# A second attention in fixed slots: one PSUM bank for inputs, one for results, later evictions, and one layer norm in place of two

## The chip, the core and the metric

The kernel runs on one core of a Trainium2 chip (trn2). The metric is device time in microseconds of one execution, the median of the runs shown. Engines are named as the profile names them: PE is TensorE (PEld its weight loads), DVE is VectorE, ACT is ScalarE, POOL is GpSimd, SP is SyncE, which issues most of the DMAs.

## The reference, cut to what matters

Four blocks in a row on x of shape (16, 256, 256): an attention with shared keys (L0), a mixture of 8 experts with the two best taken (L0), a second attention (L1), and a permuted set of small experts (L1). The change touches the third block, and the end of the second, which the kernel has merged into it. The outer layer norm and the one inside the attention follow on each other, with nothing between them:

```python
x = x + _L0_ffn_ref(_layernorm(x), ...)          # y rows of two experts, weighted, added to x
x = x + _L1_xattn_ref(_layernorm(x), ctx_1024, ...)

def _L1_xattn_ref(x, context, ln_gamma, ln_beta, w_q, w_kv, w_out, b_out, gate):
    xn = _layernorm(x, ln_gamma, ln_beta)         # eps 1e-5, as the outer one
    q = (xn @ w_q)                                # 16 heads of 64
    k, v = split(context @ w_kv)
    attn = softmax(q * 64**-0.5 @ k^T)            # per head 256 x 256
    out = (attn @ v) @ w_out + b_out
    return out * tanh(gate[0])
```

## The kernel before, in words

The work is cut into phases with a meeting of all engines between them (`phase_end`, L189). The phase concerned is the second attention: `pe_l1` (L1125), `dve_l1` (L1185), `act_l1` (L1268), `pool_l1` (L1292), `sp_l1` (L1325). Keys and values of all 16 batch entries were projected earlier and lie in DRAM. X (4096 x 256, fp32) stays in SBUF. A batch entry ("a batch" below) has 256 rows, that is two tiles of 128, and 16 heads, taken as 8 pairs. There are U = 128 pairs in all, and the loop runs over pairs; one turn of it is a slot.

For a pair u the steps are, in order: `s`, the scores (PE, 12 matmuls into two of three banks, L1139); the row maxima out of those banks (DVE, two instructions, L214); `e`, the exponentials with row sums (ACT, four instructions, L225); `g`, the reciprocals (DVE, L232) and the division by the sums (POOL, one instruction of 128 x 1024, L238); `t`, the transposes (PE, 8, L248) and their eviction (ACT, two, L255); `pv`, the product with the values (PE, 8 records, L1153) into bank 5, which DVE empties in two instructions, a rounded high part (L1225) and the rest (L1227). Matmuls whose operands are split into a high and a low part run as three products.

Once per batch there is other work. The expert rows are gathered by POOL (4 indirect DMAs, L1296) and added to X by DVE (`ca`, 4 instructions, L1192). Row statistics follow (`stats_dve`, L150: two of L153, two of L157, three small ones) and a reciprocal square root by three Newton steps on POOL (`newton_pool`, L167, 12 small instructions). Step `cm` normalizes into XN1 and takes statistics of the normalized rows, with a second `newton_pool`; step `p1` normalizes again, twice per tile (four instructions of L184). Then `p1b` transposes XN1 (PE, 4, L1161), scales it out of PSUM (DVE, L1244), rounds it (L1249), and POOL makes the low part (L1318). The query projections `q` come in 4 groups of 12 matmuls (L1171); ACT evicts the high part (L1286), DVE the low part (L1253). The keys `kk` are split by ACT (L1290) and POOL (L1323) in 4 parts. The results `o` of a batch are two groups of 24 matmuls (L1181), one per tile; DVE adds the bias (L1260), then gate and residual (L1263), and the statistics for the next phase.

`schedule` (L57) writes one list of steps, `seq1` (L1109), and every engine walks it in this order. The per-batch steps wait in a list `pend` and are dealt out in thirds over the places in a slot; a batch's two `o` steps go to the front of that list once its last `pv` is in. In a slot the order is `s`, `g` of the pair before, pieces, `e`, `t` of three pairs before, pieces, `pv` of four pairs before, pieces. So DVE empties a pair's values in the slot in which PE makes them, and the next row maxima stand behind that. Banks 7 and 6 serve the per-batch steps in turn (`mbank`, L144; `m1`, L1118).

Of the kernel before, what the change touches and what calls it, by code (L numbers as in the profile page):

```python
# [14 lines left out]
U = 128  # L15
EPS = 1e-5
# [40 lines left out]
def schedule(ins, outs, late):  # L57

    seq = [s for _, s in ins(0)]
    pend = deque()  # L60

    def pieces(n, at):
        while n > 0 and pend and at >= pend[0][0]:
            seq.append(pend.popleft()[1])
            n -= 1

    for i in range(U + 4):
        if i < U:
            if i % 8 == 0:
                pieces(len(pend), i)  # L70
                if i // 8 + 1 < 16:
                    pend.extend(ins(i // 8 + 1))
            seq.append(("s", i))
        if 1 <= i <= U:
            seq.append(("g", i - 1))
        n = -(-len(pend) // (8 - i % 8))
        pieces(n // 3 + (n % 3 > 0), i)
        if i < U:
            seq.append(("e", i))
        if 3 <= i <= U + 2:  # L80
            seq.append(("t", i - 3))
        pieces(n // 3 + (n % 3 > 1), i)
        if i >= 4:
            seq.append(("pv", i - 4))
            if (i - 4) % 8 == 7:
                for s in reversed(outs((i - 4) // 8)):
                    pend.insert(min(len(pend), late), (0, s))
        pieces(n // 3, i)
    pieces(len(pend), i)
    return seq  # L90


def build(nc, A, OUT):
# [33 lines left out]
    MV2 = keep("MV2", [128, 32, 2], fp32)  # L127
    RSTD = keep("RSTD", [128, 32], fp32)
    RSTD2 = keep("RSTD2", [128, 32], fp32)
# [17 lines left out]

    s_st, s_nw = sem("ln_guess"), sem("ln_newton")

    def stats_dve(e, w, k, t0, n, mv, r, src):  # L150
# [10 lines left out]
        e.tensor_scalar(v, mv[:, t0:t0 + n, 1], EPS, None, ALU.add).then_inc(s_st, 1)  # L161
# [936 lines left out]
    s_ca, s_mid, s_wh, s_wl, s_tanh = sem("moe_add"), sem("xn_mid"), sem("wqo_hi"), sem("wqo_lo"), sem("tanh")  # L1098
# [4 lines left out]
    def l1_ins(b):  # L1103
        qk = [(2 * n + 1, (f, b, n)) for n in range(4) for f in ("q", "kk")]
        order = [(0, ("p1", b)), (0, ("p1b", b)), (0, ("ca", b + 1))] + qk[0:2] + [
            (0, ("cg", b + 2)), (2, ("cm", b + 1)), (4, ("v", b))] + qk[2:]
        return [(at + 8 * (b - 1), s) for at, s in order]

    seq1 = [s for s in schedule(l1_ins, lambda b: [("o", b, 0), ("o", b, 1)], 0)  # L1109
            if not (s[0] in ("ca", "cg", "cm") and s[1] >= 16)]  # L1110
    use1, stat1 = {}, {("a", 0): len(stat0), ("m", 0): len(stat0) + 1}
    for s in seq1:
        if s[0] in ("p1b", "q", "o"):
            use1[s] = len(use1)
        if s[0] in ("ca", "cm") or s[0] == "o" and s[2] == 1:
            stat1[{"ca": "a", "cm": "m", "o": "o"}[s[0]], s[1]] = len(stat0) + len(stat1)

    def m1(s):  # L1118
        n = use1[s]
        return mbank(n), a1.s_m[n % 2], n // 2  # L1120

    def keys_read(b, n):
        return 2 * (8 * (b - 1) + 2 * n + 1) + 2

    def pe_l1(e, w):  # L1125
        for s in seq1:
            step, n = s[0], s[1]
            if step in ("p1b", "q", "o"):
                M, free, before = m1(s)
            if step == "s":  # L1130
                b, p = n // 8, n % 8
                _, ready, at = m1(("q", b, p // 2))
                w.wait_ge(ready, at + 1)
                w.wait_ge(s_kl, 4 * b + p // 2 + 1)
                w.wait_ge(a1.s_ex, 2 * n - 1)
                for lt in range(2):
                    for x, (i, j) in enumerate(PAIRS):
                        for h in range(2):
                            m = e.matmul(PS[SB[(2 * n + h) % 3]][:, lt * 256:lt * 256 + 256],  # L1139
                                         Q1[i][64 * h:64 * h + 64, p, lt * 128:lt * 128 + 128],  # L1140
                                         K1[j][64 * h:64 * h + 64, p, :], start=(x == 0), stop=(x == 2))
                            if lt == 1 and x == 2:
                                m.then_inc(a1.s_sc, 1)
            elif step == "t":
                a1.turn_pe(e, w, n)
            elif step == "pv":
                b, p = n // 8, n % 8
                w.wait_ge(d_vl[b % 2], 16 * (b // 2 + 1))
                w.wait_ge(a1.s_tv, 2 * n + 2)
                w.wait_ge(a1.s_ot, 2 * n)  # L1150
                for jt in range(2):
                    for h in range(2):
                        m = e.matmul(PS[OB][64 * h:64 * h + 64, 0:256], V1[b % 2][:, jt, (2 * p + h) * 64:(2 * p + h) * 64 + 64],  # L1153
                                     a1.PT[n % 4][h][:, jt * 256:jt * 256 + 256], start=(jt == 0), stop=(jt == 1))
                m.then_inc(a1.s_pv, 1)
            elif step == "p1b":
                w.wait_ge(s_xn1, 4 * n + 4)
                w.wait_ge(free, before)
                for cc in range(2):
                    for lt in range(2):  # L1160
                        m = e.transpose(M[:, cc * 256 + lt * 128:cc * 256 + lt * 128 + 128], XN1[:, lt, cc * 128:cc * 128 + 128], ident)  # L1161
                m.then_inc(s_xt1, 1)
            elif step == "q":
                w.wait_ge(s_wl, 2)
                w.wait_ge(s_xs, n + 1)
                w.wait_ge(free, before)
                for j in range(2):
                    c0 = (2 * s[2] + j) * 128
                    for cc in range(2):
                        for x, (wi, xi) in enumerate(PAIRS):  # L1170
                            m = e.matmul(M[:, j * 256:j * 256 + 256], W1Q[wi][:, cc, c0:c0 + 128], XNP[xi][:, cc, :],  # L1171
                                         start=(cc == 0 and x == 0), stop=(cc == 1 and x == 2))
                m.then_inc(s_qm1, 1)
            elif step == "o":
                lt = s[2]
                w.wait_ge(s_wl, 4)
                w.wait_ge(a1.s_ot, 2 * (8 * n + 8))
                w.wait_ge(free, before)
                for cc in range(8):
                    for x, (oi, wi) in enumerate(PAIRS):  # L1180
                        m = e.matmul(M[:, 0:256], OT1[n % 2][oi][:, cc, lt * 128:lt * 128 + 128], W1O[wi][:, cc, :],  # L1181
                                     start=(cc == 0 and x == 0), stop=(cc == 7 and x == 2))
                m.then_inc(s_om, 1)

    def dve_l1(e, w):  # L1185
        def c_add(b):
            for j, n in enumerate((0, 2, 1, 3)):
# [533 lines left out]
```

## Time and profile before

| | |
|---|---|
| median of 3 runs | 2496.23 us (2491.17 to 2498.06) |
| the profiled execution | 2494.75 us, its span 2493.0 us |
| busy share of the span | PE 79%, PEld 65%, DVE 62%, ACT 45%, POOL 41% |
| mean granted TensorE clock | 0.883 of full speed |
| chain that ended last | PE 43%, DVE 36%, issue 10%, ACT 6% |

Busy shares are averages over phases with different limits; the second attention takes about a third of the span. The granted clock has two levels, 1.0 (2.4 GHz) and 0.5 (1.2 GHz); a value between them is a mean over a stretch. A row of the timeline begins with its start and its length in us; what stands in brackets is how long the engine sat idle before it and what ended that.

### The profile page before, as it was taken

The page shows a single profiled execution, that of the slowest core. Times are in us where ns is not written, and L with a number is a line of the kernel's source. Part 1 is how long each engine was busy: PE and PEld are TensorE (multiplying, and loading weights), DVE is VectorE, ACT ScalarE, POOL GpSimd, SP SyncE. Part 2 cuts the span into 40 slices and gives each one's busy share as a digit, 9 for nine tenths or more (in the row PEclk, how much of TensorE's full clock was granted, in tenths as well). Part 3 has the DMA queues.
Part 4 walks back from the last instruction along what each step waited for, and adds up shares of the span by engine and source line. Part 5 has one row for each costly group of instructions (what it writes and reads, how often), then busy time and mean ns, then how long its engine had stood idle before and what let it go on. Part 6 is the DMA issues. An engine that isn't in the chain of part 4 may idle for free.

```text
span 2493.0 us, 40687 instructions
## 1 busy us (share of the span) xinstructions
PE 1959.3 (79%) x15424; PEld 1615.4 (65%) x15424; DVE 1549.7 (62%) x2973; ACT 1128.8 (45%) x2768; POOL 1019.8 (41%) x1477
## 2 busy tenths in 40 slices
PE   5888888889479688888888737787877877887796
PEld 3555566579369688888888736666665666765572
DVE  4666666622000688888888667777777777655461
ACT  1444444523134454555454325655555565565530
POOL 1221211101610455555555357666666666553100
PEclk8788888859689899999999869989989999997999
DMA  6444344106556455555555231112111111101079
GB/s 170 108 94 106 91 106 116 44 26 222 215 187 221 163 186 182 179 178 180 176 180 176 92 114 52 60 44 68 43 60 50 61 44 59 52 1 73 35 307 335
DMA packets 141011, 302.59 MB, mean 121 GB/s; under 512 B 12688, under 2 KB 92560, under 8 KB 125712
## 3 DMA queue, kind: packets, MB, share of 16 engines
q1 hardware_dynamic: 119088, 191.94, 24.5%
q0 software_dynamic: 17376, 103.85, 12.0%
q10 hardware_dynamic: 4352, 4.20, 0.5%
q8 instruction: 122, 2.00, 0.3%
q14 instruction: 73, 0.60, 0.1%
HBM read 199.54 MB, written 100.14 MB: 120 GB/s over the span
## 4 chain that ended last, share of the span: by engine, by line
PE 43%; DVE 36%; issue 10%; ACT 6%; DMA 4%; POOL 1%; POOLq 0%; SPq 0%; ACTq 0%; DVEq 0%
DVE W2P L1017 6%; DVE HP L1013 5%; DVE HP L1015 4%; PE ps L730 4%; PE ps L736 4%; PE ps L1181 4%; PE ps L1139 4%; PE ps L939 3%; DVE XN L184 3%; PE ps L1153 3%; PE ps L1518 2%; DMA R<-rp_scratch 2%; DVE NM L489 2%; PE ps L1171 2%; ACT PX L1480 2%
## 5 line engine op out<-in xcount | busy, mean ns | idle before, releaser
L1032 POOL TENSOR_TENSOR W1P<-WE,W1P 128x512 fp32r<-128x512 f32 x156 | 241.3, 1550 | 297.4 <-ACT W1P L971 297.4
L939 PE MATMUL ps<-XRP,W1P 128*128 128x256 f32 x1872 | 261.4, 306 | 106.6 <-DVE XRP L1002 104.9
L225 ACT ACTIVATE P<-ps,NM 128x256 f32<-128x256 f32 x512 | 236.0, 480 | 207.7 <-DVE NM L214 205.9
L939 PEld LDWEIGHTS ps<-XRP,W1P 128*128 128x128 f32 x1872 | 253.5, 216 | 114.8 <-DVE XRP L1002 114.8
L983 ACT ACTIVATE HF<-ps,WE 128x256 f32<-128x256 f32 x312 | 131.1, 476 | 301.1 <-PE ps L939 294.6
L238 POOL TENSOR_TENSOR P<-P,RS 128x1024 f32<-128x1024 f32 x128 | 245.2, 1917 | 41.1 <-DVE RS L232 40.5
L172 POOL TENSOR_TENSOR LTMP<-RSTD 128x2 f32<-128x2 f32 (+1 forms) x204 | 41.9, 205 | 526.9 <-DVE RSTD L165 516.3
L953 PE MATMUL ps<-W2P,HP 128*128 128x256 f32 x1872 | 229.0, 281 | 0.0
L953 PEld LDWEIGHTS ps<-W2P,HP 128*128 128x128 f32 x1872 | 222.3, 188 | 0.0
L560 ACT ACTIVATE PT<-ps 128x512 f32<-128x512 f32 x256 | 138.6, 593 | 161.4 <-PE ps L380 161.2
L1013 DVE CAST HP<-HF 128x512 fp32r<-128x512 f32 x156 | 136.0, 872 | 93.6 <-ACT HF L983 93.6
L489 DVE TENSOR_REDUCE NM<-ps 128x2 f32<-128x512 f32 x256 | 164.3, 684 | 29.0 <-PE ps L369 28.9
L1153 PE MATMUL ps<-PT,V 128*64 128x256 f32 x1024 | 152.4, 422 | 37.5 <-DVE OT L1227 37.5
L214 DVE TENSOR_REDUCE NM<-ps 128x2 f32<-128x512 f32 x256 | 164.4, 684 | 24.1 <-PE ps L1139 22.0
L1017 DVE TENSOR_TENSOR W2P<-WE,W2P 128x512 fp32r<-128x512 f32 x156 | 175.8, 1127 | 0.0
L1139 PEld LDWEIGHTS ps<-K,Q 64*128 64x128 f32 x1536 | 110.4, 206 | 74.1 <-issue 46.8
L1000 DVE CAST XRP<-ps 128x512 fp32r<-128x512 f32 x39 | 26.7, 683 | 207.4 <-PE ps L926 207.4
L248 PE MATMUL ps<-CST,P 128*128 128x128 f32 x1024 | 145.3, 288 | 13.0 <-ACT PT L255 10.6
L777 ACT ACTIVATE KVS<-ps 128x512 f32<-128x512 f32 x128 | 75.4, 598 | 170.5 <-remote 62.3
L1139 PE MATMUL ps<-K,Q 64*128 64x256 f32 x1536 | 137.8, 316 | 18.5 <-ACT P L225 18.4
L255 ACT ACTIVATE PT<-ps 128x512 f32<-128x512 f32 x256 | 141.1, 619 | 19.5 <-PE ps L248 19.5
L1015 DVE TENSOR_TENSOR HP<-HF,HP 128x512 fp32r<-128x512 f32 x156 | 134.4, 861 | 5.4
(198 smaller groups left out, 4128.0 us busy)
## 6 DMA issues: line engine op xcount, KB each, us to landing
k_scratch<-KVS SPq DMA_DIRECT2D x64, 256.0 KB
v_scratch<-KVS SPq DMA_DIRECT2D x64, 256.0 KB
KS<-k_scratch SPq DMA_DIRECT2D x16, 1024.0 KB, 4.8
V<-v_scratch SPq DMA_DIRECT2D x16, 1024.0 KB
rp_scratch<-RP SPq DMA_DIRECT2D x32, 512.0 KB
R<-rp_scratch SPq DMA_DIRECT2D x16, 1024.0 KB, 13.8
QS<-q_scratch SPq DMA_DIRECT2D x96, 128.0 KB, 4.6
xs_scratch<-ZERO SPq DMA_DIRECT2D x13, 768.0 KB, 7.8
```

The lines of the kernel that those rows point to most:

```text
L214: e.tensor_reduce(self.NM[:, u % 4, 2 * x:2 * x + 2], PS[SB[n % 3]][:, :].rearrange("p (h j) -> p h j", h=2), AX.X, ALU.max, negate=True). ...
L225: i = e.activation(self.P[u % 4][:, c, :], PS[SB[n % 3]][:, y * 256:y * 256 + 256], ACT.Exp, bias=self.NM[:, u % 4, c:c + 1], accum_out=se ...
L238: e.tensor_tensor(p, p, self.RS[:, u % 4, :].unsqueeze(2).to_broadcast([128, 4, 256]), ALU.mult).then_inc(self.s_pn, 1)
L489: e.tensor_reduce(NM0[b % 2][:, :, 8 * h + p], PS[SB[(2 * n + h) % 3]][:, :].rearrange("p (l j) -> p l j", l=2), AX.X, ALU.max, negate=Tru ...
L939: m = e.matmul(PS[p][:, hh * 256:hh * 256 + 256], W1P[i % 2][wi][:, cc * 1024 + hc * 128:cc * 1024 + hc * 128 + 128], XRP[i % 2][xi][:, cc ...
L953: m = e.matmul(PS[4 + k][:, s * 256:s * 256 + 256], HP[k][hi][:, hc, s * 128:s * 128 + 128], W2P[k][wi][:, hc * 256:hc * 256 + 256], start ...
L1013: e.tensor_copy(hi, HF[p % 2][:, :]).then_inc(s_hp, 1)
L1015: e.tensor_tensor(lo, HF[p % 2][:, :], hi.bitcast(fp32), ALU.subtract).then_inc(s_hp, 1)
L1017: e.tensor_tensor(W2P[j % 2][1][:, 512 * p:512 * p + 512], WE2[j % 2][:, 512 * p:512 * p + 512], W2P[j % 2][0][:, 512 * p:512 * p + 512].b ...
L1032: e.tensor_tensor(W1P[i % 2][1][:, 512 * p:512 * p + 512], WE1[i % 2][:, 512 * p:512 * p + 512], W1P[i % 2][0][:, 512 * p:512 * p + 512].b ...
L1139: m = e.matmul(PS[SB[(2 * n + h) % 3]][:, lt * 256:lt * 256 + 256], Q1[i][64 * h:64 * h + 64, p, lt * 128:lt * 128 + 128], K1[j][64 * h:64 ...
L1153: m = e.matmul(PS[OB][64 * h:64 * h + 64, 0:256], V1[b % 2][:, jt, (2 * p + h) * 64:(2 * p + h) * 64 + 64], a1.PT[n % 4][h][:, jt * 256:jt ...
```

## The change

The list is gone. Each engine has a loop over slots i, with g = i // 8 and r = i % 8, and what a slot holds per batch is written out. Two layer norms become one: with m and v the mean and variance of a row, the second norm's factor times the first's is 1 / sqrt(v (1 + eps) + eps^2) (`twice` in `stats_dve`), so the second statistics, the second Newton steps and four of the six normalizing instructions (L184) of a batch go. Bank 7 (QB) takes the transposes and all four query groups of a batch in turn; bank 6 (RB) takes the results, of which each group of 24 matmuls is issued in two halves in different slots. DVE empties a pair's values one slot later, first thing in its slot. ACT evicts the transposes one slot later, first thing in its slot. The four adds, the statistics, the gathers and the key splits have slots of their own. The buffers MV2 and RSTD2 go. In the diff below, the three loops are PE's, DVE's and ACT's, in this order.

```diff
+    QB, RB = PS[7], PS[6]
+    s_qb, s_rb = a1.s_m
+    SLOTS = U + 19
+    def use_x(b):
+        return 5 * b - 1 if b else 0
+    def use_q(b, n):
...
+        return QB, s_qb, 5 * b + n
...
+        for i in range(SLOTS):
+            g, r = i // 8, i % 8
+            if i < U:
+                scores(i)
...
+            if 0 <= i - 3 < U:
+                a1.turn_pe(e, w, i - 3)
+            if r == 0 and is_batch(g - 2):
+                result(g - 2, 0, 1)
+            elif r == 1 and is_batch(g):
+                queries(g, 3)
+            elif r == 2:
+                if is_batch(g + 1):
+                    turn_x(g + 1)
+                if is_batch(g - 2):
+                    result(g - 2, 1, 0)
+            elif r == 3 and is_batch(g - 2):
+                result(g - 2, 1, 1)
+            elif r == 4 and is_batch(g + 1):
+                queries(g + 1, 0)
+            elif r == 5 and is_batch(g - 1):
+                result(g - 1, 0, 0)
+            elif r == 6 and is_batch(g + 1):
+                queries(g + 1, 1)
+            elif r == 7 and is_batch(g + 1):
+                queries(g + 1, 2)
+            if 0 <= i - 4 < U:
+                values(i - 4)
...
+        for i in range(SLOTS):
+            g, r = i // 8, i % 8
+            if 0 <= i - 5 < U:
+                values_split(i - 5)
+            if i < U:
+                a1.max_dve(e, w, i)
+            if 0 <= i - 1 < U:
+                a1.recip_dve(e, w, i - 1)
+            if i == 1 or r == 0 and 1 <= g < 16:
+                queries_low(g, 2)
+            if r == 0 and is_batch(g + 1):
+                norms(g + 1)
+            elif r == 1 and is_batch(g - 2):
+                result_add(g - 2, 0)
+            elif r == 2 and is_batch(g):
+                queries_low(g, 3)
+            elif r == 3 and is_batch(g + 1):
+                scale_x(g + 1)
+            elif r == 4:
...
+                    result_add(g - 2, 1)
...
+                    add(g + 2, 0)
+            elif r == 5:
...
+                    queries_low(g + 1, 0)
...
+                    add(g + 2, 1)
+                    add(g + 2, 2)
+            elif r == 6 and is_batch(g + 2):
+                add(g + 2, 3)
+                stats_x(g + 2)
+            elif r == 7:
...
+                    queries_low(g + 1, 1)
...
+                    stats_out(g - 2)
...
+        for i in range(U + 4):
+            if i >= 4:
+                a1.turn_act(e, w, i - 4, i - 7)
...
+            if i < U:
+                a1.exp_act(e, w, i)
+            if r == 0 and is_batch(g):
+                keys_high(g, 2)
...
```

POOL's slot is the division of the pair before (`norm_pool(i - 1)`), then: r = 0 and 1, `keys_low` and a gather; r = 2, the Newton steps of a finished batch; r = 3, `input_low`; r = 4, `keys_low`; r = 5, a gather; r = 6, the Newton steps of the batch after the next; r = 7, `keys_low` and a gather. ACT's query evictions (r = 0, 2, 5, 7) stand ahead of the exponentials, its key splits (r = 0, 1, 4, 7) behind them. Ahead of the loops, DVE makes the low parts of the query weights before it normalizes batch 0 and those of the result weights after that; POOL gathers batch 1 and splits the first keys before it makes batch 0's low input. SP loads the keys of a batch once the key splits of the batch before are done, and values two batches deep.

## Rows read from the trace of the kernel before

**Rows 1.** Two stretches: us; PE, PEld, DVE, ACT, POOL busy; granted clock; DMA share, GB/s.
```profile
1473.55:2220.53 746.98, 598.32 (x5001) 472.86 (x5000) 559.99 (x1236) 427.86 (x1382) 486.07 (x779) 0.92 0.15 53
...
1638.24:2077.79 439.55, 350.58 (x2917) 276.89 (x2917) 334.08 (x739) 245.89 (x792) 290.60 (x478) 0.92 0.16 55
```

**Rows 2.** Chain that ended last, 1740 to 1775 us: start, length, what.
```profile
1741.76 2.74 PE ps L1181 x24
1744.49 1.01 PE ps L1153 x8
1745.51 0.90 PE ps L1139 x12
1746.41 1.61 PE ps L1171 x12
1748.02 0.87 PE ps L248 x8
...
1766.12 1.91 PE ps L1153 x8
```

**Rows 3.** Waits, 1638 to 2078 us: total us, times, longest.
```profile
PE ps L1161 <- DVE XN L184: 36.1, 9, 4.0
...
PE ps L1153 <- DVE OT L1227: 24.7, 17, 2.3
...
PE ps L1181 <- DVE OT L1227: 13.7, 10, 1.8
```

**Rows 4.** Groups of instructions, 1638 to 2078 us: count, busy us, mean ns, idle before.
```profile
L238 POOL TENSOR_TENSOR P<-P,RS 128x1024 f32<-128x1024 f32 x72 | 138.2, 1920 | 18.3 <-DVE RS L232 18.1
...
L1192 DVE SCALAR_TENSOR_TENSOR X<-GY,W,X 128x256 f32<-128x256 f32 x36 | 29.5, 879 | 0.0
L184 DVE TENSOR_SCALAR XN<-X,MV,RSTD 128x256 f32<-128x256 f32 x36 | 26.8, 763 | 0.0
L1253 DVE TENSOR_TENSOR Q<-ps,Q 128x512 fp32r<-128x512 f32 x36 | 24.5, 681 | 16.1 <-ACT Q L1286 16.1
...
L1263 DVE SCALAR_TENSOR_TENSOR X<-TMP,TG,X 128x256 f32<-128x256 f32 x18 | 22.7, 1264 | 0.6
...
L184 DVE TENSOR_SCALAR XN<-XN,MV,RSTD 128x256 f32<-128x256 f32 x18 | 20.5, 1138 | 0.7
```

**Rows 5.** Timeline of DVE and POOL from 1768 us.
```profile
1768.08 0.42 DVE L1225 CAST OT<-ps 128x256 fp32r<-128x256 f32 x1 [0.46 <-PE ps L1153]
...
1769.13 1.29 DVE L214 TENSOR_REDUCE NM<-ps 128x2 f32<-128x512 f32 x2 [0.17 <-PE ps L1139]
1770.33 0.17 DVE L232 RECIPROCAL RS<-SM 128x4 f32<-128x4 f32 x1
1770.42 3.28 DVE L1192 SCALAR_TENSOR_TENSOR X<-GY,W,X 128x256 f32<-128x256 f32 x4
...
1770.58 2.04 POOL L238 TENSOR_TENSOR P<-P,RS 128x1024 f32<-128x1024 f32 x1 [1.59 <-DVE RS L232]
...
1773.73 0.75 DVE L153 BATCH_NORM_STATS2 ST<-X 128x6 f32<-128x256 f32 x2
...
1775.21 0.17 DVE L165 TENSOR_SCALAR RSTD<-LTMP 128x2 int32<-128x2 int32 x1
```

**Rows 6.** Line L1192 by itself, whole span: ns shortest/median/longest, first and last start.
```profile
L1192 DVE SCALAR_TENSOR_TENSOR X<-GY,W,X x64: 451/473/2121, 1432.3 to 2114.7; 128x256 f32<-128x256 f32 x64
```

**Rows 7.** Timeline, 2200 to 2203 us: maxima of a pair, then the next scores.
```profile
2200.19 1.29 DVE L214 TENSOR_REDUCE NM<-ps 128x2 f32<-128x512 f32 x2
...
2202.16 0.77 PEld L1139 LDWEIGHTS ps<-K,Q 64*128 64x128 f32 x12 [0.39 <-ACT P L225]
```

**Rows 8.** A stretch of 2 us, columns as in Rows 1.
```profile
1766.00:1768.00 2.00, 2.00 (x11) 0.82 (x10) 1.42 (x3) 0.00 (x0) 0.30 (x1) 0.50 0.13 53
```

**Rows 9.** Timeline ahead of the first pair.
```profile
1454.94 0.41 DVE L184 TENSOR_SCALAR XN<-X,MV,RSTD 128x256 f32<-128x256 f32 x1 [3.12 <-POOL RSTD L178]
...
1461.04 6.05 PE L1171 MATMUL ps<-XNP,W1Q 128*128 128x256 f32 x36 [3.23 <-POOL XNP L1318]
```

More of the change, by code:

```diff
@@ L54, in __call__ @@
         return t
[L57 to L90, printed above, removed]
 def build(nc, A, OUT):
@@ L1123, in keys_read, with use_o, scores_read @@
+    def use_o(b, lt):
+        return 1 + 2 * b + lt
+    def scores_read(b, n):
         return 2 * (8 * (b - 1) + 2 * n + 1) + 2
     def pe_l1(e, w):
[L1126 to L1135, printed above, removed]
-                for lt in range(2):
[L1137 to L1158, printed above, removed]
-                for cc in range(2):
[L1160 to L1182, printed above, removed]
-                m.then_inc(s_om, 1)
@@ L1185, in dve_l1, with scores @@
[L1185 to L1192 removed]
+        def scores(u):
+            b, p = u // 8, u % 8
+            _, ready, at = use_q(b, p // 2)
+            w.wait_ge(ready, at + 1)
+            w.wait_ge(s_kl, 4 * b + p // 2 + 1)
+            w.wait_ge(a1.s_ex, 2 * u - 1)
+            for lt in range(2):
+                for x, (i, j) in enumerate(PAIRS):
+                    for h in range(2):
+                        m = e.matmul(PS[SB[(2 * u + h) % 3]][:, lt * 256:lt * 256 + 256],
+                                     Q1[i][64 * h:64 * h + 64, p, lt * 128:lt * 128 + 128],
+                                     K1[j][64 * h:64 * h + 64, p, :], start=(x == 0), stop=(x == 2))
+                        if lt == 1 and x == 2:
+                            m.then_inc(a1.s_sc, 1)
@@ new lines, in values @@
+        def values(u):
+            b, p = u // 8, u % 8
+            w.wait_ge(d_vl[b % 2], 16 * (b // 2 + 1))
+            w.wait_ge(a1.s_tv, 2 * u + 2)
+            w.wait_ge(a1.s_ot, 2 * u)
+            for jt in range(2):
+                for h in range(2):
+                    m = e.matmul(PS[OB][64 * h:64 * h + 64, 0:256], V1[b % 2][:, jt, (2 * p + h) * 64:(2 * p + h) * 64 + 64],
+                                 a1.PT[u % 4][h][:, jt * 256:jt * 256 + 256], start=(jt == 0), stop=(jt == 1))
+            m.then_inc(a1.s_pv, 1)
@@ new lines, in turn_x, with queries @@
+        def turn_x(b):
+            w.wait_ge(s_xn1, b + 1)
+            w.wait_ge(s_qb, use_x(b))
+            for cc in range(2):
+                for lt in range(2):
+                    m = e.transpose(QB[:, cc * 256 + lt * 128:cc * 256 + lt * 128 + 128], XN1[:, lt, cc * 128:cc * 128 + 128], ident)
+            m.then_inc(s_xt1, 1)
+        def queries(b, n):
+            M, free, before = use_q(b, n)
+            w.wait_ge(s_wl, 2)
+            w.wait_ge(s_xs, b + 1)
+            w.wait_ge(free, before)
+            for j in range(2):
+                c0 = (2 * n + j) * 128
+                for cc in range(2):
+                    for x, (wi, xi) in enumerate(PAIRS):
+                        m = e.matmul(M[:, j * 256:j * 256 + 256], W1Q[wi][:, cc, c0:c0 + 128], XNP[xi][:, cc, :],
+                                     start=(cc == 0 and x == 0), stop=(cc == 1 and x == 2))
+            m.then_inc(s_qm1, 1)
@@ new lines, in result @@
+        def result(b, lt, half):
+            w.wait_ge(s_wl, 4)
+            w.wait_ge(a1.s_ot, 2 * (8 * b + 8))
+            w.wait_ge(s_rb, use_o(b, lt))
+            for cc in range(4 * half, 4 * half + 4):
+                for x, (oi, wi) in enumerate(PAIRS):
+                    m = e.matmul(RB[:, 0:256], OT1[b % 2][oi][:, cc, lt * 128:lt * 128 + 128], W1O[wi][:, cc, :],
+                                 start=(cc == 0 and x == 0), stop=(cc == 7 and x == 2))
+            if half:
+                m.then_inc(s_om, 1)
```

322 lines of the change are left out of this document (179 added, 143 removed).

## The prediction

> **What bounds the kernel now.** I read the stretches first, then the chain of waits inside the second attention, then its waits and its groups. From the first scores to the last, the loop over 128 pairs takes 747 us [rows 1]. Nine batches in its middle (from one batch's results to those nine later) take 439.55 us, 48.84 each, and no engine fills that: per batch PE is busy 38.95, DVE 37.12, POOL 32.3 and ACT 27.3 us. So order and waiting are the bound, and 9.9 us per batch are PE's idle time.
>
> Where nothing waits, the chain runs through PE alone: 1.01 for the values, 0.91 for the scores, 1.61 for a query group, 0.87 for the transposes, 4.41 us in all, and 2.74 for a group of results [rows 2]. At this speed a batch needs 8 x 2.79 + 4 x 1.61 + 2 x 2.74 us, with 0.45 for its own four transposes (half of 0.87): 34.7 us. PE's busy 38.95 is 4.2 more, because after waits the clock falls to its low level: eight records of the values then take 1.91 [rows 2], in a stretch granted 0.50 [rows 8]. So a batch is 34.7 of work, 4.2 of slow clock, 9.9 of waiting. The waiting is mostly three things: for the normalized rows (36.1 / 9 = 4.0 us per batch) and for the evicted values, ahead of the next values (2.7) and ahead of the results (1.5) [rows 3].
>
> **What the change removes.** On DVE per batch two normalizations of 0.763 and two of 1.138 us [rows 4], two statistics (0.75 for both) and five small instructions of about 0.17 [rows 5]: 5.4 us. On POOL 12 Newton instructions go. Both were partly beside PE, so I credit no sum of them; what counts is which wait remains. The wait for normalized rows goes: they are made in r = 0 and first needed in r = 2. The two waits for evicted values go: DVE empties a pair right after PE's slot, and PE wants the bank 3 us later. The transposes are evicted a slot late, but first thing on ACT, while PE does that slot's scores.
>
> **What it adds.** One bank serves five uses in turn, and the next use waits until DVE has taken the low part of the one before. Twice the two lie in the same slot. In r = 2 the transposes wait for `queries_low(g, 3)`; in r = 7 `queries(g + 1, 2)` waits for `queries_low(g + 1, 1)`. Behind that waiting instruction stands the whole of PE's queue: that slot's values and the next scores. The Trainium skill, Perfetto Trace Analysis, section Matmul Optimizations, speaks against this: it wants all eight PSUM banks used, so that more can run side by side. The list of waits of before, from which three stand in [rows 3], names no wait of PE for a query bank in these batches, so the alternation had it free; I take the loss, and price it so.
>
> DVE's time in a slot: emptying 0.9 us, maxima 1.2, reciprocal 0.2 [rows 5], 2.3 in all. A query's low part is 0.68 and reads PSUM [rows 4]; back to back I take 0.65. What counts besides is that DVE instructions reading only SBUF stop while POOL works: an add alone takes 0.45 [rows 6], but four took 3.28 us beside POOL's division of 2.04, the first ahead of it [rows 5], and the means of 0.879 and 1.264 for L1192 and L1263 [rows 4] say that this is usual. In the new slots POOL's division (1.92) starts just when the reciprocal ends, and such work follows it. So a slot's first such instruction, if a PSUM one is ahead of it, ends 2.05 us after the reciprocal; one straight behind the reciprocal slips in, as in [rows 5], at 0.45.
>
> *To the wait in r = 7*, counted from the end of the scores of r = 4. DVE: r = 4, 1.4 + 2.05 + 0.45 (result add, one add; 1.35 if POOL's key split gets in first) = 3.9 to 4.8; r = 5, 2.3 + 2.05 + 0.45 (low part, two adds) = 4.8; r = 6, 2.3 + 0.45 + 1.5 (an add, and statistics as from 1773.73 to 1775.21 [rows 5]) = 4.25; r = 7, 2.3 + 0.65 = 2.95. Sum 15.9 to 16.8. PE: 3.5 to end r = 4, 4.16 (half a result group) for r = 5, 4.41 for r = 6, 1.78 to its queries: 13.85. The wait is 2.05 to 2.95 us.
>
> *To the wait in r = 2*, from the start of r = 0, where DVE has caught up (it waits for the last values). DVE: 0.95 + 1.4 + 2.05 + 0.41 (or 1.3) in r = 0 (two normalizations), 0.9 + 1.4 + 2.05 in r = 1, 2.95 in r = 2: 12.1 to 13.0. PE: 4.16 + 4.41 + 1.78 = 10.35. The wait is 1.75 to 2.65 us.
>
> If DVE's SBUF work met no POOL work, each wait would be 0.95 + 1.4 + 0.65 - 1.78 = 1.2. That is the lower end; the rows lie near the upper. Together I take 4.7 us per batch. Maxima that start late also delay scores: from the start of a pair's maxima to the next scores 1.97 us pass [rows 7], so DVE may lag by 1.5 in a slot of 4.4 before PE feels it; my slots come to about that.
>
> The clock: 9.9 us of waiting go with 4.2 of slow clock, so 4.7 go with 2.0; I take 1.6, since fewer waits may not each lower it (ends 0, and 4.2 as now).
>
> **Costed at nothing.** POOL, busy 32.3 per batch now [rows 1] (issuing gathers not counted), gets lighter by a Newton round; its division has nearly two slots until PE transposes. Without that cover r = 2 and r = 6, a division of 1.92 [rows 4] and a Newton round of about 3.1 (DVE's wait for one in [rows 9]), would cost 0.5 apiece. SP's queue: keys go out after the last split of the batch before, values after the last product two batches back, some two slots apart in a batch, so neither holds the other. ACT has 27.3 us of work in 41; were its evictions of the transposes late, PE would lose some tenths in a slot. Gathers keep their number and go out seven slots ahead.
>
> **The sum.** A batch: 34.7 + 4.7 + 1.6 = 41.0 instead of 48.84. From the first scores to the last: 18.5 until r = 3 of batch 0 (no values yet), 38 for that batch (no results), 13 x 41, 39 for the batch without adds, 14.5 for the last slots: 643 against 747, 104 less. Ahead of it, normalized rows of batch 0 waited for a second Newton round until 1454.94 and the first queries started at 1461.04 [rows 9]; without that round, with gathers still ahead of the low input, I put the queries 7.5 us earlier and the first scores, no longer behind three query groups, 15 earlier. At the end three half groups of batch 14 are left over: 3 us more. Together 104 + 15 - 3 = 116. The profiled execution took 2494.75 us with its span of 2493.0, 1.5 below the median of 2496.23: 2379 by its own time, 2380 beside the median.
>
> **Rivals.** *The ports cost little* (20%): POOL's division starts late enough, or DVE early enough, that both waits are 1.2 us and the clock holds. A batch is 34.7 + 2.4 = 37.1, 14 batches save 55 more: 2325. For it: the lighter DVE load; against: the means in [rows 4].
>
> *The single banks bind harder* (17%): key splits get in ahead of adds, both waits are at 5.6 together and the clock costs 4.2 as now. A batch is 44.5: 2380 + 14 x 3.5, or 2429. For it: the serial sums above have no spare; against: r = 3 and r = 0 let DVE catch up.
>
> *The order moves, the time doesn't* (3%): DVE, 37.12 - 5.4 = 31.7 us of old means per batch, is held off so often that the waits come back elsewhere, 12.5 us of them. A batch is then 34.7 + 1.6 + 12.5, as before, and the time about 2489.
>
> *Slower* (5%): short waits in so many slots that the clock stays low. At the low level the chain's pieces are 1.91 / 1.01 as long [rows 2], 65.6 us per batch; with a share f of work at that level a batch is 34.7 + 30.9 f + 4.7, and the change loses from 49.8 us on, f = 0.34. The granted clock is 0.92 now [rows 1], f about 0.16 of the time, and waiting is halved, which speaks against it. With f = 0.5, 54.9 us and 2575. The Trainium skill, TensorE: Matmul & The Clock Gate, section on psum-queue depth-cycling, tells of a kernel in which brief idling between groups as banks are cycled made the clock swing; no row here shows it without a wait.
>
> **How the numbers follow.** The forecast has 55%, its own range 2345 (waits 3.8, no slow clock: 38.5) to 2415 (5.6 and twice 1.6: 43.5). The range 2330 to 2435 leaves out half of the first rival, the last two, and little of the second. A difference of 0.3% (7.5 us) is about what a measurement of this kernel can tell. Faster by more: 0.55 + 0.2 + 0.17, 0.92; within: 0.03; slower: 0.05.
>
> **What the new profile would show.** Right: about 41 us per batch; no wait of PE for XN or for evicted values in the list; PE's largest waits on DVE's low query parts, one at the transposes and one at the queries, about 2 us each; L1192 and L1263 still well over 0.5; granted clock 0.95 or more; first scores about 1458 us. Wrong: waits of PE at the scores on ACT, or at the transposes on POOL, longer than those; a clock under 0.85; a batch over 45 us.

## The result: 2417.7 us, and the profile after

The changed kernel takes 2417.70 us in the median of four runs (2415.56 to 2418.55); the kernel before, beside it, 2497.14 (2491.17 to 2499.20). The ratio is 0.9684, 95% interval 0.9666 to 0.9703: 79 us less. The forecast was 2380 in a range of 2330 to 2435, so sign and range hold and of the forecast gain of 116 us a third was missing. The profiled execution took 2418.55 us with a span of 2416.8. In all that follows, one execution of four of the last version (e936), which took 5078.43 us, is left out as slow.

The stretch of twelve batches of the changed kernel, from one batch's normals to those twelve later (columns as in [rows 1]), and PE's list of waits in it (total us, times, longest):

```profile
1553.43:2075.57 522.14, 457.90 (x3890) 368.80 (x3889) 458.02 (x854) 328.32 (x1057) 361.10 (x479) 0.94 0.18 61
```

```profile
PE ps L1146 <- DVE Q L1229: 27.2, 12, 2.3
PE ps L1134 <- DVE Q L1229: 18.6, 12, 1.6
PE ps L214 <- ACT PT L221: 18.2, 38, 0.9
```

A batch is 522.14 / 12 = 43.51 us, against 48.84 [rows 1] and a forecast of 41.0. The waits for normals and for evicted values [rows 3] are gone. In their place stand the two the prediction named, on bank 7's low parts: 2.27 us a batch at the queries (slot 7, L1146) and 1.55 at the transposes of the rows (slot 2, L1134). The third, 1.5 us a batch on ACT's evictions of the transposed probabilities, it had costed at nothing.

PE's timeline in one batch of the changed kernel shows what stands behind each long wait (last, in brackets, the idle time and what ended it), and two windows give the granted clock there (third from the end: 0.76 and 0.60):

```profile
1734.76 1.06 PE L214 MATMUL ps<-CST,P 128*128 128x128 f32 x8 [0.60 <-ACT PT L221]
1737.37 0.67 PE L1134 MATMUL ps<-CST,XN 128*128 128x128 f32 x4 [1.55 <-DVE Q L1229]
1737.75 2.86 PE L1156 MATMUL ps<-W1O,OT 128*128 128x256 f32 x12
1740.54 1.40 PE L1125 MATMUL ps<-PT,V 128*64 128x256 f32 x8
...
1743.63 1.62 PE L1156 MATMUL ps<-W1O,OT 128*128 128x256 f32 x12
1745.18 1.08 PE L1125 MATMUL ps<-PT,V 128*64 128x256 f32 x8
...
1764.31 2.28 PE L1146 MATMUL ps<-XNP,W1Q 128*128 128x256 f32 x12 [2.27 <-DVE Q L1229]
1766.51 1.98 PE L1125 MATMUL ps<-PT,V 128*64 128x256 f32 x8
```

```profile
1739.30:1743.30 4.00, 4.00 (x32) 2.98 (x31) 1.26 (x3) 0.00 (x0) 1.90 (x10) 0.76 0.21 82
1764.30:1768.30 4.00, 3.99 (x20) 2.75 (x20) 3.78 (x7) 2.75 (x8) 3.68 (x6) 0.60 0.00 0
```

Behind the wait of 1.55 a half group of results takes 2.86 us where the next takes 1.62; behind the wait of 2.27 the values take 1.98 for 1.08. So in this batch each wait costs some 1.5 us again. It is not so in every batch. In the twelve batches a wait of 1.55 was followed by such a fall in eight and one of 2.27 in ten. In the batch of 1632.91 the queries behind the same 2.27 took 1.68, the values 1.08.

Why DVE is late is on its own timeline, slots 1 and 2 of the batch shown:

```profile
1730.96 1.28 DVE L180 TENSOR_REDUCE NM<-ps 128x2 f32<-128x512 f32 x2
1732.15 0.17 DVE L198 RECIPROCAL RS<-SM 128x4 f32<-128x4 f32 x1
1732.24 0.39 DVE L1244 TENSOR_TENSOR TMP<-ps,BO 128x256 f32<-128x256 f32 x1
1732.66 1.91 DVE L1247 SCALAR_TENSOR_TENSOR X<-TMP,TG,X 128x256 f32<-128x256 f32 x1
...
1735.28 1.28 DVE L180 TENSOR_REDUCE NM<-ps 128x2 f32<-128x512 f32 x2
...
1736.56 0.66 DVE L1229 TENSOR_TENSOR Q<-ps,Q 128x512 fp32r<-128x512 f32 x1
```

POOL's division in the same stretch:

```profile
1732.40 1.89 POOL L204 TENSOR_TENSOR P<-P,RS 128x1024 f32<-128x1024 f32 x1 [1.16 <-DVE RS L198]
```

The reciprocal of 1732.15 releases POOL's division, and the second add, whose two inputs both lie in SBUF, takes 1.91 us beside it and ends 0.3 after it; the one ahead of it, fed from PSUM, takes 0.39. The low part for which PE waits begins that much later. Two rows of ACT show the third wait: the exponentials (L191) stand idle for late maxima, and the eviction of the transposes (L221) stands behind them (and a key split) in ACT's queue:

```profile
1731.67 0.48 ACT L191 ACTIVATE P<-ps,NM 128x256 f32<-128x256 f32 x1 [2.07 <-DVE NM L180]
...
1734.00 1.09 ACT L221 ACTIVATE PT<-ps 128x512 f32<-128x512 f32 x2
```

DVE's groups over the twelve batches (count, busy us, mean ns) show the stops everywhere:

```profile
L1201 DVE SCALAR_TENSOR_TENSOR X<-GY,W,X 128x256 f32<-128x256 f32 x48 | 49.4, 1048 | 0.0
L1247 DVE SCALAR_TENSOR_TENSOR X<-TMP,TG,X 128x256 f32<-128x256 f32 x24 | 45.8, 1908 | 0.8
...
L150 DVE TENSOR_SCALAR XN<-X,MV,RSTD 128x256 f32<-128x256 f32 x25 | 36.7, 1507 | 0.0
...
L127 DVE TENSOR_SCALAR LTMP<-MV 128x2 f32<-128x2 f32 x12 | 18.7, 1559 | 0.4
L116 DVE BATCH_NORM_STATS2 ST<-X 128x6 f32<-128x256 f32 x48 | 17.9, 415 | 0.4
```

L1201 alone takes 0.45 [rows 6], and the second result add had a mean of 1.264 before [rows 4]: the fixed slots put SBUF work behind the reciprocal every time, so it is now held more, not less.

### The profile page after: what moved, and what is told of

Read it like the earlier page. It is cut to its first block, busy times and chain, and to the rows that moved or that the text cites. A ratio compares the mean times of both kernels' runs of the same rounds, so it can differ in the third digit from the quotient of the medians.

```text
span 2416.8 us, 40302 instructions
## 1 busy us (share of the span) xinstructions
PE 1947.3 (81%) x15424; PEld 1611.4 (67%) x15424; DVE 1550.8 (64%) x2797; ACT 1130.1 (47%) x2768; POOL 990.0 (41%) x1285
## 4 chain that ended last, share of the span: by engine, by line
DVE 43%; PE 36%; issue 8%; ACT 5%; DMA 4%; POOL 2%; another core or an unknown queue 2%; POOLq 0%; SPq 0%; DVEq 0%; ACTq 0%
DVE W2P L983 7%; DVE HP L979 5%; DVE NM L180 5%; DVE HP L981 4%; PE ps L696 4%; PE ps L702 3%; PE ps L905 3%; DVE NM L455 2%; DMA R<-rp_scratch 2%; ACT PX L1576 2%; DVE X L1201 2%; PE ps L356 2%; PE ps L1125 2%; PE ps L1614 2%; DVE X L1247 2%
## 5 line engine op out<-in xcount | busy, mean ns | idle before, releaser
L191 ACT ACTIVATE P<-ps,NM 128x256 f32<-128x256 f32 x512 | 235.6, 473 | 236.9 <-DVE NM L180 236.8
L138 POOL TENSOR_TENSOR LTMP<-RSTD 128x2 f32<-128x2 f32 (+1 forms) x156 | 31.2, 200 | 451.9 <-DVE RSTD L131 443.8
L214 PE MATMUL ps<-CST,P 128*128 128x128 f32 x1024 | 139.3, 279 | 23.4 <-ACT PT L221 23.4
L1146 PE MATMUL ps<-XNP,W1Q 128*128 128x256 f32 x768 | 119.6, 311 | 45.4 <-DVE Q L1229 37.8
L1125 PE MATMUL ps<-PT,V 128*64 128x256 f32 x1024 | 146.3, 409 | 0.0
L221 ACT ACTIVATE PT<-ps 128x512 f32<-128x512 f32 x256 | 140.1, 612 | 3.7 <-PE ps L214 3.7
L1146 PEld LDWEIGHTS ps<-XNP,W1Q 128*128 128x128 f32 x768 | 106.8, 211 | 50.2 <-DVE Q L1229 41.6
L214 PEld LDWEIGHTS ps<-CST,P 128*128 128x128 f32 x1024 | 110.0, 141 | 43.8 <-issue 18.2
```

What stands on the lines that cost most here:

```text
L191: i = e.activation(self.P[u % 4][:, c, :], PS[SB[n % 3]][:, y * 256:y * 256 + 256], ACT.Exp, bias=self.NM[:, u % 4, c:c + 1], accum_out=se ...
L214: i = e.transpose(PS[TB[h]][:, c0:c0 + 128], self.P[u % 4][:, c, jt * 128:jt * 128 + 128], ident)
```

## The experiments

Two theories stood at the start. **W**: what a batch takes above PE's own work comes from DVE reaching the low parts late, and the slow clock follows those waits. Against it, that the dropped layer norm is nearly all of the gain and the order gives little. Times below are "gains": the kernel before in the same set of runs minus the kernel tried, medians. The changed kernel's own gain is 79. The kernel before took 2498.72, 2499.47 and 2501.47 us beside the first, third and last set of runs; beside the second set it took 2428.76, so there the batches are compared (more on this at the end).

### The layer norm alone (e1)

To the kernel before:

```diff
-            (0, ("cg", b + 2)), (2, ("cm", b + 1)), (4, ("v", b))] + qk[2:]
+            (0, ("cg", b + 2)), (4, ("v", b))] + qk[2:]
...
-            stats_dve(e, w, stat1["a", b], 2 * b, 2, MV, RSTD, lambda t: X[:, t, :])
+            stats_dve(e, w, stat1["a", b], 2 * b, 2, MV, RSTD, lambda t: X[:, t, :], True)
...
-                    normal(e, XN1[:, lt, :], XN1[:, lt, :], t, MV2, RSTD2).then_inc(s_xn1, 1)
```

> The kernel before with the one layer norm alone: its list of steps, whole result groups and eager emptying stay, the second statistics, square root and normals are gone. Theory W (what a batch of eight slots lost before lies in waits for the normals, for the low parts of the attention results and for result adds that stand in a bunch; the norm removes the first of these alone): the 36.1 us of waits for the normals over nine batches, 4.0 a batch, fall by half or more, the other waits stay, so a batch takes 46 to 47 us in place of 48.8 and the time is 2455 to 2470. Rival N (the dropped norm is the gain and the order of slots adds little): 2430 or less. Rival O (the norm is worth nothing, since DVE's list only fills the room with other steps): 2488 or more.

Measured: 2438.43 us, ratio 0.977 (0.9731 to 0.9809), gain 60. Twelve batches and PE's longest waits in them:

```profile
1542.66:2088.67 546.01, 461.22 (x3888) 364.55 (x3888) 411.06 (x853) 328.07 (x1058) 354.26 (x489) 0.93 0.16 58
```

```profile
PE ps L1164 <- DVE XN L187: 38.9, 12, 3.2
PE ps L1156 <- DVE OT L1220: 25.1, 16, 2.4
```

A batch is 45.5 us, half a us under W's 46 to 47, and the time falls between W and N. So of the 79 us the norm brings 60 (48 to 67 by the interval) and the slots the rest, some 19; the slots without the shorter norm were not tried. The waits for normals did not halve (3.24 a batch, 4.0 before); what shrank is the rest. The slots then remove these two waits, 5.3 us a batch, and some shorter ones, and put 5.3 of their own in their place (3.8 for low parts, 1.5 for ACT): PE idles 85 us in e1's twelve batches, 64 in the changed kernel's.

### Low parts ahead of the maxima (e3), and the add out of SBUF (e4)

To the changed kernel, e3 and then e4:

```diff
                 values_split(i - 5)
+            if r == 2 and is_batch(g):
+                queries_low(g, 3)
+            if r == 7 and is_batch(g + 1):
+                queries_low(g + 1, 1)
             if i < U:
                 a1.max_dve(e, w, i)
...
-            elif r == 2 and is_batch(g):
-                queries_low(g, 3)
...
-                if is_batch(g + 1):
-                    queries_low(g + 1, 1)
```

```diff
             w.wait_ge(s_rb, use_o(b, lt))
+            w.wait_ge(s_xa, 2 * b + lt)
             for cc in range(4 * half, 4 * half + 4):
...
-            e.tensor_tensor(TMP1[:, 0:256], RB[:, 0:256], BO[:, :], ALU.add).then_inc(s_rb, 1)
+            e.tensor_tensor(RB[:, 0:256], RB[:, 0:256], BO[:, :], ALU.add).then_inc(s_rb, 1)
-            e.scalar_tensor_tensor(xv, TMP1[:, 0:256], TG[:, 1:2], xv, ALU.mult, ALU.add).then_inc(s_xa, 1)
+            e.scalar_tensor_tensor(xv, RB[:, 0:256], TG[:, 1:2], xv, ALU.mult, ALU.add).then_inc(s_xa, 1)
```

The added wait of e4 is PE's: bank 6 now holds the result until the second add has read it.

> The changed kernel with the two low query parts that share a bank with PE's next product (slots 2 and 7 of a batch) moved ahead of their slot's maxima. Theory W (the 1.55 and 2.27 us a batch that PE waits on them come from DVE's order, and the fall of the clock behind each wait comes with them): both waits shrink by 1.2 us or more, the batch of 43.5 us loses 2.4 to 4.5, the time is 2356 to 2384. Rival D (the scores' maxima, now 0.45 us later in these slots, are due as well, so that PE waits for the exponentials or transposes instead): the wait only changes its name, 2410 or more.

> The changed kernel with the result's bias added in place in PSUM, so that the second add reads one input from PSUM and has one in SBUF: it should no longer stand still beside the division on POOL (1.91 us in two of three cases, 0.48 in the third). Theory C (contention of DVE's SBUF-only instructions with the division delays the low part behind them): this add takes 0.4 to 0.5 us throughout, the wait of the transposes of slot 2 on the low part of slot 2 falls from 1.55 to under 0.5, that of slot 7 by some tenths, and the time is 2375 to 2395. Rival S (the stop moves to the next SBUF-only instruction in DVE's order, and the low part is as late as before): the add is short, the waits stay within 0.3 us, 2412 to 2422.

Measured: e3 2378.01 us, gain 121; e4 2370.23, gain 128 (ratios 0.9513, 0.9483, each within 0.004). Twelve batches of e3, then of e4 with its waits and the add's group:

```profile
1510.20:2002.00 491.80, 434.22 (x3888) 345.43 (x3884) 446.39 (x844) 329.06 (x1060) 364.55 (x471) 1.00 0.19 65
```

```profile
1549.20:2026.89 477.69, 434.94 (x3890) 349.99 (x3889) 425.26 (x854) 326.84 (x1057) 358.92 (x479) 0.99 0.19 67
```

```profile
PE ps L1146 <- DVE Q L1230: 20.2, 12, 1.7
PE ps L214 <- ACT PT L221: 14.4, 20, 0.9
PE ps L1134 <- DVE Q L1230: 7.6, 12, 0.6
```

```profile
L1248 DVE SCALAR_TENSOR_TENSOR X<-ps,TG,X 128x256 f32<-128x256 f32 x24 | 11.6, 483 | 0.9
```

e3 went W's way. The two waits fall to 0.6 and 1.0 us and the clock stays at 1.00 throughout; some of it comes back on ACT, as rival D had it. e4 went theory C's way and further: its time is 5 us under C's range, though the wait of slot 2 fell to 0.63, not under 0.5. In e4 two instructions of a batch (all 24 of the stretch stood still before, not two of three) lose 1.4 us each of standing still, and the batch loses 3.7: 39.8. This is the contention shown with one input moved. e4's clock fell behind four of its twelve waits of 1.68, and behind none of 0.63.

### Emptying at the end of the slot (e5)

```diff
-            if 0 <= i - 5 < U:
-                values_split(i - 5)
             if i < U:
                 a1.max_dve(e, w, i)
...
+            if 0 <= i - 4 < U:
+                values_split(i - 4)
```

> The changed kernel with one part undone: DVE empties the bank of the attention results at the end of the slot in which PE filled it, not at the start of the next. Theory W (at the end of the slot DVE stands waiting for PE's product, and the maxima of the next slot, the reciprocal and all behind it begin later): the batch grows by 1 to 3 us, 2435 to 2460. Rival H (the place of the emptying is of no matter, since in program order only the step of the slot changes sides with it): within 8 us of 2418.

Measured: 2413.40 us, gain 85; a batch is 43.54 us, the waits the same within 0.1 us a batch. This was a badly chosen experiment: the end of a slot and the start of the next are the same place in DVE's order, so theory W had no ground to expect a loss. What it gives is how far two kernels with the same order lay apart, 4 to 6 us, most of it ahead of the second attention. What the later emptying alone is worth was not measured.

### Both, and the other parts undone (e34, e6, e7, e346)

e34 is e3 and e4 together. The edit of e6 (PE's loop), then that of e7 (DVE's; POOL's first gather moves from slot 5 to 7 with it); e346 is e34 with e6's:

```diff
             if r == 0 and is_batch(g - 2):
+                result(g - 2, 0, 0)
                 result(g - 2, 0, 1)
...
-                if is_batch(g - 2):
-                    result(g - 2, 1, 0)
             elif r == 3 and is_batch(g - 2):
+                result(g - 2, 1, 0)
                 result(g - 2, 1, 1)
...
-            elif r == 5 and is_batch(g - 1):
-                result(g - 1, 0, 0)
```

```diff
-                if is_batch(g + 2):
-                    add(g + 2, 0)
...
-                if is_batch(g + 2):
-                    add(g + 2, 1)
-                    add(g + 2, 2)
             elif r == 6 and is_batch(g + 2):
-                add(g + 2, 3)
+                for j in range(4):
+                    add(g + 2, j)
```

> The edits of e3 and e4 together: both same-slot low query parts ahead of the maxima, and the result's bias added in PSUM. In e4 a batch still has 3.5 us of waiting, 1.7 of it for the low part of slot 7, 0.6 for that of slot 2 and 1.2 for ACT's evictions of the transposes; PE is busy 36.2 a batch. Theory W (the low parts are the chief waits, and each edit takes a different share of them): the low-part waits fall to 0.5 a batch or less, 1.2 to 2 on ACT stay, a batch is 37.5 to 38.5, the time 2335 to 2355. Rival D (as in e3, what the low parts give up comes back as waits for ACT, since the maxima are later): a batch stays at 39.5 or more, 2366 or more.

> The changed kernel with one part undone: the results in whole groups of 24 products, in slots 0 and 3, no halves. Theory W (DVE's late low parts set the waits, and the place of PE's own work only moves them): slot 5 is 1.57 us shorter for PE, so the wait of slot 7 grows from 2.27 to about 3.8; slot 0 is 1.57 longer, so that of slot 2 goes from 1.55 to about nothing; the batch keeps 43 to 44 us, 2408 to 2430. Rival E (even slots are what the halves pay with: a slot with 24 products lets ACT and DVE run idle, and the short ones then wait): 2435 or more.

> The changed kernel with one part undone: the four adds of gathered rows in one bunch in slot 6, ahead of the statistics, in place of one, two and one in slots 4, 5 and 6 (POOL's gather that waits for the first of them is issued two slots later). Theory W (in slots 4 to 7 DVE is behind PE all the way, so only the sum of its work there counts; in either order one add of 0.45 slips in ahead of a division and one of 1.9 stands beside it): the wait of slot 7 stays within 0.6 us of 2.27 and the time within 8 us of 2418. Rival P (the bunch delays the maxima of slot 7 and all behind them, as four adds in a bunch did in the kernel before): 2430 or more.

> The kernel of e34 with the results in whole groups of 24 products, in slots 0 and 3. With the low parts early there is less for the place of PE's work to move. Theory W: the wait of slot 7 grows by about 1.5 us a batch and that of slot 2 has nothing to give, 10 to 25 us slower than e34. Rival R (halves cost PE: a whole group takes about 2.9 us of the trace of e1, two halves 2 x 1.57, and the fall of the clock is gone either way): as fast as e34 or up to 7 us faster.

Measured, with the kernel before at 2428.76: e34 2307.98 (gain 121), e6 2335.92 (93), e7 2365.74 (63), e346 2311.82 (117); batches 40.28, 42.6, 44.2 and 40.23. Eleven batches of e34, PE's waits on ACT in them, and the stops that are left in it:

```profile
1521.83:1964.93 443.10, 397.99 (x3566) 317.70 (x3568) 381.86 (x782) 299.94 (x969) 332.70 (x450) 1.00 0.19 66
```

```profile
PE ps L214 <- ACT PT L221: 21.7, 22, 1.0
...
PE ps L1112 <- ACT P L191: 6.5, 12, 0.6
```

```profile
1682.86 2.91 DVE L150 TENSOR_SCALAR XN<-X,MV,RSTD 128x256 f32<-128x256 f32 x2
...
1717.59 1.55 DVE L127 TENSOR_SCALAR LTMP<-MV 128x2 f32<-128x2 f32 x1
1719.18 1.21 DVE L129 TENSOR_SCALAR LTMP<-LTMP 128x2 int32<-128x2 int32 x1
```

Rival D was right on e34: with the low parts early, the normals of slot 0 and the small steps of slot 7 still stop for some 4.5 us together, the maxima behind them are late, and PE waits for ACT. Where the low parts stand is not the cause; that DVE stops is.

e7 went rival P's way, not W's: the gain is 16 us smaller, and the wait of slot 7 grew from 2.27 to 3.60 (four adds take 3.28 us in a bunch, as in [rows 5]), so spreading them is worth some 0.7 us a batch. e6 missed W's range on the other side: whole groups are about 0.9 us a batch faster than halves, and the wait of slot 7 stayed at 2.27 in place of growing, since PE now waits 1.2 us for ACT and DVE earlier in the batch; that of slot 2 fell only to 1.2. With the low parts early (e346) halves and whole groups are equal within 4 us, nearer to rival R than to W.

### The division released last (e9, e8, e86)

e9 is the changed kernel, e8 is e4, e86 is e4 with e6's edit, each with this (DVE's loop):

```diff
-            if 0 <= i - 1 < U:
-                a1.recip_dve(e, w, i - 1)
             if i == 1 or r == 0 and 1 <= g < 16:
                 queries_low(g, 2)
...
                 if is_batch(g - 2):
                     stats_out(g - 2)
+            if 0 <= i - 1 < U:
+                a1.recip_dve(e, w, i - 1)
```

> The changed kernel with one thing moved: DVE takes the reciprocal, which releases POOL's division, as its last step of a slot, behind the slot's other work, no longer right behind the maxima. Theory C (DVE's instructions with nothing but SBUF operands stand still because the division runs beside them, and a division that starts later runs beside the emptying and the maxima, which read PSUM): normals fall from 1.5 to about 0.45 us apiece, the second result add from 1.9 to about 0.5, adds from 1.05 to about 0.5; the low-part waits (3.85 us a batch) fall under 1, the clock holds, a batch is 36.5 to 39.5 in place of 43.5, and the gain on the kernel before is 79 + 14 times 4 to 7, 135 to 175 us. Rival S (other POOL work, its splits of keys above all, meets the same instructions, or a later division makes ACT and the transposes late): a batch of 41 or more, gain under 115.

> e4 (result's bias added in PSUM) with the reciprocal as the last step of a slot. Theory C: of e4's 3.5 us of waits a batch most goes, a batch is 36.5 to 38.5 in place of 39.8, the gain on the kernel before 145 to 175 us. It should differ little from e9, since an add that no longer stops needs no input in PSUM. Rival S: 39.5 or more, gain under 132.

> e8 with the results in whole groups of 24 products in slots 0 and 3. Theory H (what halves cost PE, some 0.2 a group, is all that is left to see, as from e34 to e346): within 6 us of e8. Rival E (with DVE no longer late the even slots are what keeps ACT and POOL in step): 10 us or more slower than e8.

Measured: e9 2348.58 us, ratio 0.9406 (0.9384 to 0.9427), gain 151; e8 2349.39, gain 150; e86 2342.02, ratio 0.9373 (0.9341 to 0.9404), gain 157. Twelve batches of e9, PE's waits and DVE's groups in them:

```profile
1545.42:2007.80 462.38, 430.71 (x3888) 346.13 (x3888) 339.66 (x853) 326.97 (x1056) 355.21 (x479) 1.00 0.21 69
```

```profile
PE ps L1134 <- DVE Q L1229: 12.5, 12, 1.0
PE ps L1146 <- DVE Q L1229: 11.4, 12, 1.0
PE ps L1146 <- POOL XNP L1371: 7.7, 12, 0.6
```

```profile
L1201 DVE SCALAR_TENSOR_TENSOR X<-GY,W,X 128x256 f32<-128x256 f32 x48 | 21.9, 476 | 0.0
L116 DVE BATCH_NORM_STATS2 ST<-X 128x6 f32<-128x256 f32 x48 | 17.9, 415 | 0.4
...
L1247 DVE SCALAR_TENSOR_TENSOR X<-TMP,TG,X 128x256 f32<-128x256 f32 x24 | 11.7, 488 | 0.8
...
L150 DVE TENSOR_SCALAR XN<-X,MV,RSTD 128x256 f32<-128x256 f32 x24 | 9.1, 418 | 0.0
...
L127 DVE TENSOR_SCALAR LTMP<-MV 128x2 f32<-128x2 f32 x12 | 2.0, 169 | 0.4
```

Theory C holds. The same instructions with the same operands take 0.42 in place of 1.51, 0.49 for 1.91, 0.48 for 1.05, 0.17 for 1.56 us, because the division now runs beside the emptying (L1235, L1237) and the maxima, which read PSUM. In one slot of e9, from POOL's and DVE's timelines:

```profile
1585.06 1.90 POOL L204 TENSOR_TENSOR P<-P,RS 128x1024 f32<-128x1024 f32 x1
1585.56 0.42 DVE L1235 CAST OT<-ps 128x256 fp32r<-128x256 f32 x1 [0.77 <-PE ps L1125]
```

DVE's busy time falls from 38.2 to 28.3 us a batch, the batch by 5.0 to 38.5, and the clock is 1.00. Of the 5.0, 2.7 are PE's idle time and 2.3 its busy time, in the main the slow clock. What was off: each low part still costs 1.0, where I had expected under 1 for both. e8 confirms that e4's edit adds nothing once the add doesn't stop. e86 came out 7 us faster than e8, 0.6 us a batch: nearer to H than to E, and the halves bring nothing here either.

### The best version (e936)

It is e9, with e6's whole groups and e3's early low parts.

> The reciprocal last in a slot (e9), the results in whole groups (e6), and the two same-slot low query parts ahead of the maxima (e3). In e86 a batch of 37.95 us has 2.4 us of waiting, 2.0 of it for these two low parts (1.04 and 0.95), and PE is busy 35.6. Theory W: each of the two falls to about 0.4 and nothing takes their place, now that DVE has no stops to hand on: a batch is 36.4 to 37.2, the gain on the kernel before 167 to 180 us. Rival D (as from e4 to e34, later maxima come back as waits for ACT): a batch of 37.9 or more, gain under 160.

Measured: 2330.55 us in the median of three executions (2323.65 to 2336.27), ratio 0.9313 (0.926 to 0.9367), gain 171. A batch is 443.54 / 12 = 36.96 us; twelve of them, and PE's longest waits:

```profile
1543.21:1986.75 443.54, 428.79 (x3891) 344.92 (x3890) 347.99 (x853) 325.62 (x1057) 358.05 (x481) 1.00 0.21 72
```

```profile
PE ps L214 <- ACT PT L221: 10.6, 24, 0.5
```

Theory W's batch and gain hold: the wait of slot 2 falls to 0.2 us a batch and that of slot 7 is gone. But something did take their place: PE's waits for ACT's evictions are 0.9 a batch, where they are 0.4 in e86. PE is busy 35.7 of the 37.0 us: the second attention is bound by PE at last. This version beats both kernels.

## Why the prediction was right, and where its terms were off

**Right.** The three waits of [rows 3] went; the two on bank 7's low parts came where it put them, r = 7 larger than r = 2; SBUF-only work met the division in every slot; the rest of the kernel stayed. The page it weighed, the Trainium skill, Perfetto Trace Analysis, Matmul Optimizations (use all eight banks), spoke of a real loss: 3.8 us a batch for one bank with five uses. But e936 keeps the single banks, and its waits for their low parts are 0.2 us a batch; so it was the late release that cost, not the single bank. Two banks in turn were not tried with these slots.

**The batch, term by term** (forecast, measured):

- PE's work 34.7, 36.2 (e3: 434.22 / 12 at a granted clock of 1.00). This term was too small. Part of it is a reading: the group of results that has 2.74 on the chain of [rows 2] takes 2.91 on PE's timeline, from its start at 1741.51 to the values at 1744.42, which makes 0.3 a batch. Halves for whole groups are another 0.3 (e8 35.9, e86 35.6). The pieces were also read where each runs straight into the next; ahead of a wait the end of a step counts as busy too (the transposes last 1.09, and where work follows at once it starts 0.85 after them). An estimate for e3, with some three waits a batch behind transposes at 0.24 and some three behind other steps at 0.07, is 0.9, which leaves nothing large open.
- Low-part waits 4.7, 3.8 (2.27 inside its bounds of 2.05 to 2.95, 1.55 just under 1.75). The chain of slot 4 to slot 7 took DVE 17.0 us in the batch shown (maxima at 1747.22 to the end of the low part at 1764.25), a little over the 15.9 to 16.8 of the sum; PE took 14.9 for 13.85, 0.7 of it in waits for ACT. Both came out longer than forecast, so it is in part luck that their difference fell inside its bounds.
- Transposes on ACT's evictions "some tenths in a slot", costed at nothing; 1.5 (38 waits of 0.5 in twelve batches). This was the wrong step: the cover it named was ACT's free time, but the evictions stand in ACT's queue behind exponentials that wait for late maxima.
- Slow clock 1.6, 2.0 (38.16 busy less 36.2).

That makes 43.5 for 41.0. The forecast's own range also ends at 43.5 a batch, but made of longer low-part waits and twice the slow clock; that the wider range held owes something to luck. Over the loop, from first to last scores, it is 674.8 us (1466.2 to 2141.0) for a forecast of 643, 747 before. Ahead of it the first scores came 7 us earlier, not 15: they came as early after the mixture's end as forecast, but that phase, whose instructions are the same, ended 7 us later in this execution. In e5, with the same instructions too, the first scores start at 1459.3, so this is the spread between executions. The tail cost 3.3 for 3. Together 72.2 + 7.3 - 3.3 = 76 of span, for 116.

**The rivals.** "The ports cost little" named its own condition: each wait is 1.2 us when SBUF work meets no POOL work. e9 makes that so, and the waits are 1.04 and 0.95; the time was not 2325 but 2349, in the main since PE's work had been put 1.2 us a batch too low in every case, and since e9 adds a wait of 0.6 for POOL. "The single banks bind harder" had a batch of 44.5 and 2429, nearer to the result than the forecast, though not by its cause: the waits did not reach 5.6. "The order moves, the time doesn't" and "Slower" never came near: the waits are 5.3 us a batch, not 12.5, and the clock is 0.94.

## What to carry to other kernels

Here the adds, normals and casts of DVE with all their operands in SBUF were priced by what POOL did beside them, not by their own length; the row statistics were not. Before splitting work or adding buffers, look at which instruction releases POOL, and release it when DVE has only PSUM work ahead: here one moved line was worth some 70 us, nearly as much as the whole rewrite. When one wait of PE is removed, ask who else waits in the queue of the engine that was late: in e34 the waits came back through ACT.

## What was not expected of the hardware

**Which instructions stop.** Beside the division, normals, casts, adds of two SBUF inputs and even a scalar step of 128 x 2 (0.17 to 1.56 us) wait for its end, while the row statistics, which also read only SBUF, take 415 ns in the changed kernel and in e9 alike. The prediction had it of all DVE work that reads only SBUF. POOL's key split stops such steps as well: in the changed kernel the small step of 1766.82 ran until 1768.01, the split until 1767.98. The Trainium skill, SBUF — State Buffer, section "SBUF: two separate sides", has the pair of ports that DVE and GpSimd share as an exclusive lock for a whole instruction, taken by a DVE instruction of two SBUF inputs or in a mode of two ports. The runs agree: with one of the two inputs moved to PSUM (e4) the add takes 0.48 us beside the same division. Whether the normals and casts ran in such a mode, no run here shows.

**The clock.** The granted clock fell behind eight of twelve waits of 1.55 us and ten of twelve of 2.27 in the changed kernel, behind four of twelve of 1.68 in e4, and behind none of e9's, which are 1.04, 0.64 and 0.95 in a batch. So here several short waits cost their own length, and a long one often more. What decides between two equal waits is open.

**A faster stretch in one set.** In the set of e34 the kernel before is 70 us faster. The stretch from 640 to 720 us, in which keys and values are projected, of e34 and then of the changed kernel:

```profile
640.00:720.00 80.00, 80.00 (x519) 73.29 (x518) 0.00 (x0) 34.44 (x58) 46.56 (x48) 1.00 0.93 334
```

```profile
640.00:720.00 80.00, 30.69 (x116) 22.20 (x115) 0.00 (x0) 8.01 (x15) 50.24 (x52) 0.57 0.45 160
```

The same instructions keep PE busy in one and leave it idle for 50 us in the other, with half the traffic. The chip by itself doesn't explain it: e936 ran on a chip of the same number as e34, 1, there the kernel before took 2501.47, and e936's PE is busy for 31.46 of these 80 us. The cause stays open; the stretch lies outside the change and is in both kernels alike.
